# Fetching and splitting a stage's first weights inside the stage before it, and sharing the last residual add of a row between two engines

## The reference, cut to what matters

```python
x = x + _layernorm(_L0_attn_ref(_layernorm(x), Wq, bq, Wk, bk, Wv, bv, Wo, bo))      # 32 heads of 16, causal
x = x + _layernorm(_L0_ffn_ref(_layernorm(x), ...))    # silu(x Wg) * (x Wu), then Wd; 1792 hidden, rank-4 scaled weights
x = x + _layernorm(_L1_attn_ref(_layernorm(x), ...))   # a state-space layer: projection, short convolution, 64 heads, scan
x = x + _layernorm(_L1_ffn_ref(_layernorm(x), ...))    # 1376 hidden
return x
```

## Time and profile before

| | us |
|---|---|
| median of 3 runs (4201.26 to 4205.95) | 4203.76 |
| the profiled execution, its own time | 4211.65 |
| its span, first to last instruction | 4209.6 |

### The profile page before, as it was taken

One profiled execution on the slowest core, in us unless ns is written; L12 is line 12 of the kernel. 1 busy time (PEld: TensorE's weight loads), 2 busy tenths in 40 slices (PEclk: granted clock), 3 DMA queues, 4 the chain that ended last, 5 costly groups with the idle time before them and its releaser, 6 DMA issues.

```text
span 4209.6 us, 61612 instructions
## 1 busy us (share of the span) xinstructions
PE 3867.7 (92%) x18088; PEld 2818.5 (67%) x18088; DVE 2758.7 (66%) x5102; ACT 1705.1 (41%) x3555; POOL 1814.9 (43%) x1977
## 2 busy tenths in 40 slices
PE   6889899889999999989978998997999999999797
PEld 4444478567777777767754445885777777777676
DVE  3567455677777777764536673556777777777646
ACT  1344321355555555542213443113555545555412
POOL 1111334356556655543211114442665556655532
PEclk8687799999999999999976777998999999999999
DMA  3221011011100110002032210110111000100111
GB/s 74 56 37 32 30 47 46 20 38 29 33 20 25 35 33 27 25 1 80 23 75 56 38 30 29 54 39 25 34 33 30 28 25 25 35 28 23 36 53 35
DMA packets 84630, 151.95 MB, mean 36 GB/s; under 512 B 16488, under 2 KB 18616, under 8 KB 84432
## 3 DMA queue, kind: packets, MB, share of 16 engines
q1 hardware_dynamic: 82320, 145.38, 13.1%
q10 hardware_dynamic: 2112, 4.19, 0.3%
HBM read 119.37 MB, written 4.19 MB: 29 GB/s over the span
## 4 chain that ended last, share of the span: by engine, by line
PE 72%; issue 8%; DVE 8%; ACT 4%; DVEq 2%; POOL 2%; POOLq 1%; DMA 1%; SPq 1%; ACTq 1%; PEldq 0%; PEld 0%
PE banks L520 16%; PE banks L521 15%; PE banks L522 15%; PE banks L928 5%; PE banks L764 4%; PE banks L745 4%; PE banks L721 3%; PE banks L921 2%; DVE conv L1575 2%; PE banks L941 2%; DVEq L1578 1%; PE banks L863 1%; PE banks L864 1%; ACT conv L1128 1%; DVE conv L1572 1%
## 5 line engine op out<-in xcount | busy, mean ns | idle before, releaser
L1575 DVE SCALAR_TENSOR_TENSOR conv<-banks,cpar,conv 128x509 f32<-128x509 f32 (+2 forms) x576 | 428.6, 744 | 113.3 <-ACT conv L1128 98.2
L1094 ACT ACTIVATE probs<-banks 128x1024 f32<-128x1024 f32 (+3 forms) x384 | 298.8, 809 | 315.1 <-PE banks L745 313.7
L1908 POOL TENSOR_SCALAR_AFFINE_SELECT probs<-probs 128x256 f32<-128x256 f32 x256 | 104.0, 406 | 663.4 <-ACT probs L1094 663.0
L721 PE MATMUL banks<-stack_k,stack_q 48*128 48x512 f32 (+3 forms) x768 | 326.2, 495 | 60.6 <-DVEq L1467 20.0
L1355 DVE TENSOR_TENSOR Y<-banks,Y 128x512 f32<-128x512 f32 x368 | 253.2, 691 | 160.9 <-PE banks L522 159.5
L1973 POOL TENSOR_TENSOR state<-state,gt 128x512 f32<-128x512 f32 x112 | 134.1, 1197 | 507.6 <-PE banks L921 507.6
L520 PE MATMUL banks<-xhi,f_hi 128*128 128x512 f32 x800 | 324.4, 405 | 30.9 <-POOL f_lo L1778 16.6
L520 PE MATMUL banks<-xhi,wx_hi 128*128 128x512 f32 x768 | 314.2, 409 | 6.8 <-DVE conv L1575 6.6
L521 PE MATMUL banks<-xhi,f_lo 128*128 128x512 f32 x800 | 319.5, 399 | 0.0
L522 PE MATMUL banks<-xlo,f_hi 128*128 128x512 f32 x800 | 319.4, 399 | 0.0
L521 PE MATMUL banks<-xhi,wx_lo 128*128 128x512 f32 x768 | 308.2, 401 | 0.0
(11 more groups left out here) (217 smaller groups left out, 10174.5 us busy)
## 6 DMA issues: line engine op xcount, KB each, us to landing
m_raw<-in_w_mamba SPq DMA_DIRECT2D x224, 256.0 KB, 2.6
f_raw<-in_w_ffn SPq DMA_DIRECT2D x50, 768.0 KB, 4.6
stack_q<-part_hi SPq DMA_DIRECT2D x128, 64.0 KB, 2.5
stack_k<-part_hi SPq DMA_DIRECT2D x128, 64.0 KB, 2.5
x_next<-in_x SPq DMA_DIRECT2D x6, 1024.0 KB, 8.6
wqk_raw<-in_w_attn SPq DMA_DIRECT2D x8, 512.0 KB, 3.7
stack_q<-part_lo SPq DMA_DIRECT2D x64, 64.0 KB, 2.4
stack_k<-part_lo SPq DMA_DIRECT2D x64, 64.0 KB, 2.4
```

Source lines behind the costliest of these rows:

```text
L721: r = pe.matmul(dst[:, 0:cols], stack_q[buf][base:base + ROWS, h, i * P:(i + 1) * P], stack_k[buf][base:base + ROWS, h, s * HALF:s * HALF ...
L1094: act.activation(probs[n % 2][:, 2 * p:2 * p + 2, 0:w], banks[:, 2 * p:2 * p + 2, 0:w], ACT.Exp, scale=1.0 / HD ** 0.5).then_inc(exp_done[ ...
L1575: r = dve.scalar_tensor_tensor(out=rest, in0=src[:, 0:HALF - lag], scalar=cpar[:, o:o + 1], in1=rest, op0=ALU.mult, op1=ALU.add)
```

## The change

The change moves fetches and splits across the borders of stages, and gives FFN1 memory of its own.

- **Row border.** `first_weights` (the four transfers of `wqk`, `qk_b`, `wv`, `bv`) is issued by SP once before the row loop, and then at the start of FFN1 for the next row. `first_qk` (split of `wqk`, and the mask) and `values_weights` (split of `wv`) run on POOL before the row loop, `first_qk` ahead of the two first roots; within the loop they run in FFN1, after tiles 8 and 9 and ahead of tiles 9 and 10. PE's wait for `o_zero` moves to the first value product.
- **FFN0 to MAMBA.** SP fetches `wdt` and the other step parameters, `cpar` and the first `m_raw` in FFN0. POOL splits `wdt` and the first three `wx` (`first_split`: high and low part both on POOL) between tiles 12 and 13 of FFN0, the fourth after tile 13, the fifth and sixth around the root of half 1, and the four `wg` after that; ACT's casts for these go. PE makes half 1's transposes and `steps_in(1)` after project 1, `steps_turn(1)` after project 2 and `decay_sums` after project 3. DVE does `steps_copy(0)` first and the half's `norm_lo` before its second convolution.
- **MAMBA to FFN1.** FFN1's tiles 0 and 1 are fetched when the last projection is made; POOL splits tile 0 in the last group (`split_ahead`), one matrix each after `rg` at c = 5, 6 and 7, ahead of the root, the adds and the leaving of the stage.
- **Row end.** DVE adds tiles 4 to 7, POOL tiles 0 to 3 after its last root. SP starts both transfers to `out` when all 8 tiles are added, and not ACT.

The diff, cut to its core (the new memory layout and the passing of buffer names are left out):

```diff
-        def w_place(t, m):
-            return t * 3 + m if t > 1 else (2 * t + m if m < 2 else 4 + t)
+        def w_place(i, t, m):
+            return t * 3 + m if t > 1 or i == 1 else (2 * t + m if m < 2 else 4 + t)
...
+            def first_weights():
+                sp.dma_start(wqk_raw[:], w_attn[KT:KT + 2].rearrange("n p c -> p n c")).then_inc(wqk_in, 16)
+                sp.dma_start(qk_b[:], qk_bias[0]).then_inc(wqk_in, 16)
+                sp.dma_start(wv_raw[:], w_attn[0:KT].rearrange("n p c -> p n c")).then_inc(wv_in, 16)
+                sp.dma_start(bv_sb[:], bv).then_inc(wv_in, 16)
             for h in range(2):
                 sp.dma_start(x_next[:, h * CPH:(h + 1) * CPH, :], x_half(0, h)).then_inc(x_in[h], 16)
+            first_weights()
...
-                load_qk(0)
-                sp.dma_start(wv_raw[:], w_attn[0:KT].rearrange("n p c -> p n c")).then_inc(wv_in, 16)
-                sp.dma_start(bv_sb[:], bv).then_inc(wv_in, 16)
                 ones_in(0)
...
                     load(0, 0, True)
                     load(0, 1, True)
                     if i == 1:
+                        leave(sp, b, MAMBA)
+                        enter(sp, b, FFN1)
                         for h in range(2):
                             sp.dma_start(x_next[:, h * CPH:(h + 1) * CPH, :], x_half(B - 1, h)).then_inc(x_in[h], 16)
+                        first_weights()
...
                 ffn_loads(0, w_ffn0, NF0, True)
-                leave(sp, b, FFN0)
-                enter(sp, b, STEPS_DT)
-                for dst, src in ((wdt_raw[:], w_dt), (dtb[:], dt_bias), (alog[:], a_log), (dsk[:], d_skip)):
-                    sp.dma_start(dst, src).then_inc(dt_w_in, 16)
-                leave(sp, b, STEPS_DT)
+                enter(sp, b, FFN0)
+                for dst, src in ((wdt_raw[:], w_dt), (dtb[:], dt_bias), (alog[:], a_log), (dsk[:], d_skip)):
+                    sp.dma_start(dst, src).then_inc(dt_w_in, 16)
                 sp.dma_start(cpar[:], conv_par[0]).then_inc(cpar_in, 16)
                 for n in range(CT):
                     m_load(0, n, n, n < 2)
+                leave(sp, b, FFN0)
+                enter(sp, b, STEPS_DT)
+                leave(sp, b, STEPS_DT)
...
-                leave(sp, b, MAMBA)
-                enter(sp, b, FFN1)
+                held(sp, proj_done, (b + 1) * PROJ_PER_B)
                 ffn_loads(1, w_ffn1, NF1, False)
                 leave(sp, b, FFN1)
+                held(sp, x_added, START + (b * 4 + 4) * TT)
+                for h in range(2):
+                    own = slice(h * CPH, (h + 1) * CPH)
+                    sp.dma_start(out[b].rearrange("(t p) d -> p t d", p=P)[:, own, :], X[:, own, :]
+                                 ).then_inc(out_done[h], 16)
...
-                pe.wait_ge(o_zero, b + 1)
...
+                        if t == 0 and n == 0:
+                            pe.wait_ge(o_zero, b + 1)
...
-                    if ft == 2:
+                    if ft == 1:
                         norm_turn(b * 4 + 2, 2, half(1))
                         normed(b * 4 + 2, 1)
                         steps_in(1)
+                    if ft == 2:
+                        steps_turn(1)
                     if ft == 3:
-                        steps_turn(1)
-                    if ft == 4:
                         decay_sums()
...
-                normed_y(b * 4 + 3, range(TT))
-                for h in range(2):
-                    act.wait_ge(x_added, START + ((b * 4 + 3) * TT + (h + 1) * CPH))
-                    own = slice(h * CPH, (h + 1) * CPH)
-                    act.dma_start(out[b]...).then_inc(out_done[h], 16)
+                normed_y(b * 4 + 3, range(TT))
...
+                steps_copy(0)
                 add_y(b * 4 + 1, half(1))
                 moments_x(b * 4 + 1, 1)
-                steps_copy(0)
                 first_conv(0)
+                norm_lo(b * 4 + 2, half(1))
                 first_conv(1)
                 first_silu(0)
-                norm_lo(b * 4 + 2, half(1))
...
-                add_y(b * 4 + 3, range(TT))
+                add_y(b * 4 + 3, half(1))
...
                 for par in range(2):
                     split_tile(n // 2 - 1, par)
+                    if i == 1:
+                        (first_qk, values_weights)[par](b + 1)
+                    elif par == 0:
+                        held(pool, dt_w_in, (b + 1) * 64)
+                        split(wdt_hi[:], wdt_lo[:], wdt_raw[:]).then_inc(dt_w_ready, 1)
+                        for ft in range(3):
+                            first_split(b, wx_hi, wx_lo, ft, ft)
                 if n % 2:
                     split_tile(n // 2, 0)
...
+            first_qk(0)
             root(PRE, 0, 0)
             root(PRE, 0, 1)
+            values_weights(0)
...
                 ffn(b, 0, NF0, True)
+                first_split(b, wx_hi, wx_lo, 3, 3)
                 root(POST, b * 4 + 1, 0)
...
                 leave(pool, b, FFN0)
+                first_split(b, wx_hi, wx_lo, 4, 4)
+                root(POST, b * 4 + 1, 1)
+                first_split(b, wx_hi, wx_lo, 5, 5)
                 enter(pool, b, STEPS_DT)
-                held(pool, dt_w_in, (b + 1) * 64)
-                split(wdt_hi[:], wdt_lo[:], wdt_raw[:]).then_inc(dt_w_ready, 1)
...
+                        if last and c > CPH:
+                            split_ahead(c - CPH - 1)
                         if last and c == CPH + 1:
                             root(POST, b * 4 + 2, 0)
...
+                for k in range(2):
+                    first_split(b, wg_hi, wg_lo, k, CT + k)
+                root(PRE, b * 4 + 2, 1)
+                for k in range(2, KT):
+                    first_split(b, wg_hi, wg_lo, k, CT + k)
...
                 root(POST, b * 4 + 3, 1)
+                add_y(b * 4 + 3, half(0))
```

More of the change, by code:

```diff
@@ L141, in build @@
             sb("under_ffn", [P, TT * AH * VW + 3 * KT * D + D], stack=s)
[L142 to L144 removed]
+            wf0 = [[sb(f"{n}{i}", [P, 3, D], dt, stack=s) for i in range(2)]
+                   for n, dt in (("f_raw", F32), ("f_hi", F32R), ("f_lo", F32R))]
             lr_raw = [sb(f"lr_raw{i}", [STACK, 3 * P], stack=s) for i in range(2)]
@@ L1221, in first_tanh @@
                     conv_tanh(b * PROJ_PER_B + n, n, 0)
-                held(act, cpar_in, (b * MG + 1) * 16)
-                for n in range(2):
-                    split_hi(wx_hi[:, n, :], n, 0)
                 act.wait_ge(dt_w_in, (b + 1) * 64)
@@ L1228, in _ @@
                 normed_y(b * 4 + 1, half(1))
-                for n in range(2, 4):
-                    split_hi(wx_hi[:, n, :], n, 0)
+                held(act, cpar_in, (b * MG + 1) * 16)
                 first_conv(0)
                 first_conv(1)
+                normed_x(b * 4 + 2, 2, half(1))
                 first_tanh(0)
-                normed_x(b * 4 + 2, 2, half(1))
-                split_hi(wx_hi[:, 4, :], 4, 0)
                 first_conv(2)
@@ L1256, in _ @@
                 first_tanh(5)
-                for k in range(KT):
-                    split_hi(wg_hi[:, k, :], CT + k, 0)
                 enter(act, b, MAMBA)
@@ L1821, in ffn @@
                 f = F[i]
+                f_raw, f_hi, f_lo = FFN_WEIGHTS[i]
                 def split_one(p, par, m):
@@ L1879, in _, with values_weights @@
                                    channel_multiplier=1).then_inc(mask_built, 1)
+            def values_weights(row):
+                held(pool, wv_in, row * 32 + 32)
+                split(wv_hi[:], wv_lo[:], wv_raw[:]).then_inc(wv_ready, 1)
+            first_qk(0)
+            root(PRE, 0, 0)
+            root(PRE, 0, 1)
+            values_weights(0)
+            with pool.Fori(0, B) as b:
+                enter(pool, b, ATT)
                 ring = 0
@@ L2014, in _, with split_ahead @@
                 decay_terms(0, b * (MG * TT))
+                def split_ahead(m):
+                    f = F[1]
+                    raw, hi, lo = (w[0][:, m, :] for w in FFN_WEIGHTS[1])
+                    if m == 0:
+                        held(pool, f["raw_in0"], b * ((NF1 + 1) // 2) * 16 + 16)
+                    split(hi, lo, raw).then_inc(f["w_ready"], 1)
                 m_group(0, True, False)
```

107 lines of the change are left out of this document (56 added, 51 removed).

## The result

| | before | changed |
|---|---|---|
| first timing, median of 5 runs each | 4205.95 | 4235.36, ratio 1.0083 [1.0058, 1.0107] |
| second timing (run e10), median of 17 and 12 runs | 4215.43 | 4228.59, ratio 1.0036 [1.0010, 1.0062] |
| span of the profiled execution | 4209.6 | 4244.2 |

The account below looks back on a forecast made before the run. PE, busy 92% of the span, was taken as the bound, so only its idle time can be won. Terms of -0.7 once and +3.1 per row gave +5.5: 4203.8 to 4209.3 us, range 4196 to 4220.

Parts of the forecast that it names:

- Row end and border: End of the last row: +4.2 us once, for shared adds and later transfers; border between the rows: -9.5 us.
- a rival of 0.07: POOL's adds and splits and DVE's work lock each other out: +5 us, 4214 in all; chance 0.07.
- STEPS_DT: Step-size stage after FFN0: PE starts earlier and half 1 is ready sooner, -6.5 us in each row.
- SP late by a further 3: Border of the rows: lower bound, a gain of 6.9 us if SP issues its transfers 3 us later than forecast.
- The clock, at the last tiles and the end of MAMBA: Low PE clock behind new waits: +1.4 us per row at each FFN's last tile; no clock term at MAMBA's end.
- the first rival: PE's low clock stays after new waits: 3.4 us each in the FFNs, not 1.4; 4223.7 in all; chance 0.18.
- Start of FFN1: First tiles of FFN1: PE starts earlier, then waits for half 1 of the input; -4.0 us in each row.
- POOL's queue at the last tiles: FFN0 and FFN1: moved splits delay the last tile's gate, +3.5 and +3.1 us in each row, before the clock.
- the two splits at the end of MAMBA: MAMBA's last group: two early splits ahead of work PE waits for, +4.2 us in each row; the third hidden.
- the start: Start of row 0: the first root queues behind the query/key split and mask, +4.6 us once.
- PE's jump at the border: Border of the rows: PE must jump back in its row loop, from running dry at 2105.4 to starting at 2109.6.
- POOL's idle time: Faster rival: POOL's idle time absorbs the moved work at the FFNs' last tiles, 18.8 us less, 4190.5; chance 0.13.

Follow-up runs that it names:

- e10: The changed kernel timed and traced again with no edit: ratio 1.0036 to the kernel before.
- e1: The changed kernel with all eight adds of the row end on DVE alone: 4231.29 us, ratio 1.0052 to the kernel before.
- e3: The changed kernel with three of POOL's splits in STEPS_DT moved behind the second root: 4220.02 us, ratio 1.0030 to the kernel before.
- e8: The changed kernel with all repairs together, FFN0's early splits and wv's between the last tile's up and down matrix: 4175.83 us, ratio 0.9929 to the kernel before.
- e9: The kernel of e8 with the split of wv behind the two roots for the next row: 4165.54 us, ratio 0.9893 to the kernel before.
- e6: The changed kernel with decay_sums back behind project 4 instead of project 3: 4226.74 us, one execution.
- e2: The changed kernel with POOL's early split blocks of both FFNs behind the last weight tiles: 4213.37 us, ratio 1.0012 to the kernel before.
- e7: The changed kernel with gate 1 of FFN1 waiting for sg and up 1 for hf: 4221.53 us, one execution.
- e4: The changed kernel with two of the three early splits in MAMBA's last group moved later: 4219.54 us, ratio 1.0038 to the kernel before.
- e5: The changed kernel with the first query/key split and mask behind the two first roots: 4230.31 us, one execution.

## Why the prediction was wrong

The sign of every place that was forecast was right and the sum was not: 34.6 in the trace against 5.5. Nearly all of the 29 us between them stand in four of the prediction's steps:

- **Row end and border (5.8 us; 2.4 in the trace of e10).** "DVE's half hangs on ACT ... its last add still ends near 4204.5" and "adds end at 2117.2": both took the durations of engines that work alone. Side by side, DVE's add took 1.5 and POOL's 1.6 us. The mechanism stood as a rival of 0.07 and was priced at 5 us for the whole kernel (its own terms make 6.0); the runs put it at 3.0 at the row end and up to 3.0 at the border (e1), at 6.2 in STEPS_DT (e3), and at 6.2 us of waits, 9.5 with the clock, where a long POOL instruction meets it (e8 against e9). The rule of the Trainium skill (SBUF — State Buffer, section on two separate sides) that named it agrees with these rows: `h_lo`, 0.7 us long, started behind POOL's instruction and ended behind it, after 4.83. SP's jump of 6.24 us was the other part; the forecast had it ready near 2126 by the old scale, and it came at 2147.71 - 19.0 = 2128.7, so that the bound of 6.9 for "SP late by a further 3" is what came (7.2). Behind the first scores the clock took 2.1 us more in this trace and gave 1.3 back in that of e10: this part of the miss is chance.
- **STEPS_DT (7.1 us).** "DVE's adds and moments until 810.8" was 2.3 late for the same reason. "From there on the chain ... is the same" was wrong as well: PE's new order put project 4 behind a wait for `a_all`; e6 shows that this alone was worth nothing by the second group of MAMBA. With the adds free of POOL's splits (e3) the steps are -6.7 and -5.4, for the -6.5 forecast.
- **The clock, at the last tiles and the end of MAMBA (some 11 of 12.5 us).** 1.4 us were taken for each new wait in the FFNs. Against waits of 4.01 and 3.42 the steps were 6.4, 6.5, 6.1 and 7.8, so 2.4 to 4.4 more. Of the 4.4, 1.5 stand behind a later wait of 2.88 us (2.89 in the kernel before), where only the changed kernel's matmuls ran at the low level; e2, without the new wait, has nearly the same there (+1.2). At the end of MAMBA nothing had been taken for the clock; the waits grew by 4.0 us, for 4.2 forecast, and the step was 6.4; behind the longer waits a stretch of 7 us ran at 0.52. In FFN0 the cost lies midway between the forecast and the first rival (low clock stays, 3.4 each), in FFN1 nearer the rival.
- **Start of FFN1 (4.0 us).** "Gate 0, up 0 and gate 1 ... keep it until 1902": gate 1 overwrites a bank and waits for `hf`, which stands in DVE's queue behind the adds and moments. The work queued behind the wait was asked for on POOL and not on DVE. e7 brings 3.4 back.
- **Right:** POOL's queue at the last tiles (waits of 3.5 and 3.1 forecast, 4.01 and 3.42 measured; e2; the forecast's own times give 2.9 and not 3.1), the two splits at the end of MAMBA (e4), the start (4.6 against 5.0; e5), PE's jump at the border (4.2 against 4.33). The rule of the Trainium skill (Runtime: NRT & Kernel Launch, on instruction fetch), which speaks of a target outside of the instructions that are loaded, agrees with the row loop's jump on four queues (PE 4.33, SP 6.24, POOL 3.95, DVE 4.21 us). The inner loops jump back too, and on SP, ACT, DVE and POOL of the changed kernel the next instruction follows within 0.3 us. What is loaded when no run shows.
- **The rivals.** POOL's idle time did not absorb the moved work, though it could have: e4, e8 and e9 place the same work where POOL stands still, and with the other repairs the kernel of e9 is 1.1% faster than before.

What the trace of before showed and was passed over: a row that was read for the end of MAMBA. It has an add of two SBUF tiles at 1.22 us, right beside its PSUM twin of the same size at 0.69, while POOL works; over its 128 instructions (min/median/max) it is the same.

```profile
1866.64 0.69 DVE L1658 TENSOR_TENSOR yv<-yv,banks 128x512 f32<-128x512 f32 x1 [1.34 <-ACT yv L1199]
1867.40 1.22 DVE L1661 TENSOR_TENSOR yv<-yv,xd 128x512 f32<-128x512 f32 x1
...
L1661 DVE TENSOR_TENSOR yv<-yv,xd x128: 691/1171/1354, 873.4 to 3970.7; 128x512 f32<-128x512 f32 x128
```

## What to carry to other kernels

Work that is moved into an engine's idle time belongs behind the instruction that another engine waits for next, and the trace of before names it: the changed kernel lost 28 to 36 us outside of attention, and the same splits a few instructions later, with the other repairs, won 29. Before a pass is shared by DVE and POOL, or POOL gets work beside DVE, look whether both read from SBUF with two inputs on DVE's side: then they took turns in all these rows, and DVE alone was faster. A place is best compared by the start of the same matmul in two traces: medians of a few runs here move by more than a place is worth. A step has to be read in several traces too: the border's moved by 6 us with the same code, since the clock behind a wait fell in one execution and not in another.

## What the runs showed of the hardware that was not expected

- POOL's instruction need not have two inputs to hold DVE up: DVE's `yv<-yv,xd` alone takes 0.69 us and 1.27 (median of 110) beside POOL's AFFINE_SELECT, which reads one tile. DVE's instructions that read one tile and a PSUM bank (`Y<-banks,Y`, `xlo<-banks,xhi`) stay at 0.69 beside any of them.
- SP's way back through its row loop took 6.24 us between its last transfer and the next one (4.86 in e8); PE's took 4.33, and POOL's and DVE's had taken 3.95 and 4.21 in the kernel before.
- Attention, with the same code, took 353 to 373 us in row 1 and 387 to 414 in row 0, with the same number of matmuls. The granted clock of the stretch was 0.77 in the shortest of row 0 (e7) and 0.69 in the longest (e10).
- The same wait of PE can be followed by either level of the clock: the 2.14 us of e6 by 0.57, and by 1.00 in the changed kernel.
